# A five-layer graph GRU on one core: four batches in flight, and every state turned by block transpose and device memory instead of by TensorE

## The chip, the cores and the metric

The kernel runs on one core of a Trainium2 chip. The metric is device time in microseconds of one execution, as the median of several runs. Five engines work in parallel, each through its own queue in order, and wait for one another by semaphores: TensorE (PE, with its weight loads shown as PEld), VectorE (DVE), ScalarE (ACT), GpSimd (POOL), and SyncE (SP), which here only issues DMAs.

## The reference

For each of 16 batches with 512 nodes and 128 features: a normalized graph convolution, a residual and a layer norm; then five layers of message passing with a GRU, a residual and a layer norm.

```python
adj_norm = adj / (jnp.sum(adj, axis=-1, keepdims=True) + EPS)
h_neigh = jnp.einsum('bnm,bmf->bnf', adj_norm, x)
h = jnp.einsum('bnk,ko->bno', jnp.concatenate([x, h_neigh], axis=-1), weight) + bias
x1 = layernorm(x + relu(h))

A = (adj != 0)
h = x1
for l in range(5):
    m = jnp.einsum('bnd,de->bne', h, weight[l])
    agg = jnp.einsum('bij,bid->bjd', A, m)
    gi = agg @ w_ih.T + b_ih;  gh = h @ w_hh.T + b_hh
    r = sigmoid(i_r + h_r);  z = sigmoid(i_z + h_z);  n = tanh(i_n + r * h_n)
    h = (1 - z) * n + z * h
out = layernorm(x1 + h * mask)
```

## The kernel before

**Numbers in two parts.** Each float32 operand of a matmul is kept as a rounded part (`_hi`, made by a copy on ACT) and the rest (`_lo`, made by a subtraction on DVE or POOL). A product of two such numbers is three matmuls, one after the other into the same PSUM bank (`split_product`, L1157 to L1159). The edges are 0 or 1, so the sum over neighbours takes two groups of four matmuls: `tok_hi` (L1292), then `tok_lo` (L1299). The weight of a layer and `w_ih` are multiplied once ahead of everything into `wc`.

**Units.** One layer of one batch is a unit, 80 in all. A state `h` lies with features on partitions ([128, 512]); the sum over neighbours needs it with nodes on partitions. So each unit of layer 1 to 4 first turns its state: four 128x128 transposes on PE against `ident` (L1152) into `ps_tok`, from which ACT makes `tok_hi` and DVE `tok_lo`. A unit then is, on PE: the 8 matmuls of the sum, 9 of `state_products` (`ps_hn`, and the state's part of `ps_r` and `ps_z`), and 9 with `agg_hi`/`agg_lo` (the rest of `ps_r`, of `ps_z`, and `ps_in`). ACT makes `agg_hi`, `r_gate`, `z_gate` and the tanh in `ps_in`; DVE makes `agg_lo`, `r_hn`, two steps in `ps_in` and the new `h`; POOL makes `z_h` and the state's low part `h_lo`; ACT makes `h_hi`.

**Windows and slots.** The whole order is written out by hand, as one function `window(w)` per engine. A window has five slots, and each slot may hold a unit, `UNITS = ((0, 0), (1, 2), (2, 4), (0, 1), (1, 3))`: slot 0 takes layer 0 of the window's batch, slot 1 layer 2 of the batch before it, and so on, so that three batches are in flight. The last steps of a unit (tanh, new state, `h_hi`, `h_lo`) are done in the slot after it, and the state for the next slot's unit is turned between `state_products` and the nine `agg` matmuls of a slot (`next_turned`). The middle windows are one hardware loop; the first two (`FIRST_WINDOWS`) and the last (`LAST_WINDOWS`) hold fewer units.

**Work beside the units.** Window n also prepares batch n+1 (`prepares`): `adjt_hi` (ACT) and `adjt_lo` (POOL, L544) and the products `own_products` (PE, `ps_b[0]` and `ps_b[1]`) in slot 0; row sums of `adj` (ACT), neighbour sums (PE) and the edges (DVE, L948, four operations, two in slot 1 and two in slot 2) in slots 1 and 2; the residual `pre1` and its statistics (DVE) in slot 3; the norm to `x1` (DVE, L931, four operations), its parts, and its turn to the first state (`first_state`, PE into `ps_b[1]`, then `h[0]`, `h_hi[0]` by ACT and `h_lo[0]` by POOL) in slot 4. `own_products` of the next window writes over `ps_b[1]` and so waits for `s_h0`, which stands behind the copy of `ps_b[1]` to `h[0]`.

**The last state's way.** In the middle windows the state after layer 4 does not go through PE. DVE transposes its 32x32 blocks (L1131) to `last_blocks`; SP writes that to device memory (`passage`, L472), waits for the landing and reads it back by four DMAs (`last_rows`, L475), which puts the blocks in their places. DVE then multiplies by the mask and adds the residual (`pre2`, L976, four operations, in slot 1 of the next window), takes the statistics, and POOL writes `y_out`.

```python
sp.wait_ge(s_blocks, w.finished(1, 1))
sp.dma_start(passage[:], last_blocks[:]...).then_inc(s_passed, 16)
sp.wait_ge(s_passed, w.finished(16, 16))
for q in range(Q):
    sp.dma_start(last_rows[...], passage...[:, :, q, :]).then_inc(s_rows, 16)
```

SP's queue in a window: last state, `xt_in`, `adjt_in` (1 MB), output, `x_in`, `adj_in` (1 MB).

## Time and profile before

| | us |
|---|---|
| median of 3 runs | 625.32 (624.67 to 625.62) |
| the profiled execution | 624.76 |
| its span in the trace | 623.0 |
| one window of the loop | 37.0 |

The trace is of the profiled execution. Its span runs from the first to the last instruction; the 1.8 us around it belong to the time but not to the trace. Durations of PE's matmuls reach to a modelled end and overlap the next matmul, so the pace of PE is read from the starts. DVE and ACT overlap the ends of their operations a little too: two DVE operations of 0.69 us stand about 0.61 us apart.

### The profile page before, as it was taken

How to read it: one execution, taken by the hardware profiler on the slowest of the kernel's cores; microseconds unless marked ns; L12 is line 12 of the kernel's file. 1: busy time of each engine (PE TensorE's matmuls, PEld its weight loads, DVE VectorE, ACT ScalarE, POOL GpSimd, SP SyncE). 2: the span in 40 equal slices, each digit the busy share in tenths (PEclk: the TensorE clock that was granted, in tenths of full speed). 3: DMA queues.
4: the chain of work that ended last, by engine and by line, in shares of the span. 5: the costliest groups of instructions: out<-in, count | busy, mean ns of one | idle time of the engine just before them, and what ended most of it. 6: DMA issues, size and time to landing. Idle time of an engine off the chain costs nothing.

```text
span 623.0 us, 10141 instructions
## 1 busy us (share of the span) xinstructions
PE 604.4 (97%) x2877; PEld 492.6 (79%) x2877; DVE 515.1 (83%) x1177; ACT 411.3 (66%) x777; POOL 366.5 (59%) x299
## 2 busy tenths in 40 slices
PE   6999999999999999999999999999999999999993
PEld 5677888888888888888888888888888888887772
DVE  5987978897988879798897979889798887967677
ACT  4866776858667585766758576685866758564551
POOL 0644555757666575765658576576766657555343
PEclk9999999999999999999999999999999999999997
DMA  8531222231232323223231331333124131010101
GB/s 270 213 102 68 101 69 102 99 104 52 84 134 68 101 68 121 80 84 114 88 101 51 99 120 67 118 100 102 51 84 135 67 101 34 17 34 1 51 1 52
DMA packets 48080, 54.63 MB, mean 88 GB/s; under 512 B 2880, under 2 KB 27968, under 8 KB 48064
## 3 DMA queue, kind: packets, MB, share of 16 engines
q1 hardware_dynamic: 47792, 54.31, 26.3%
q8 instruction: 7, 0.11, 0.1%
q10 hardware_dynamic: 272, 0.13, 0.1%
q14 instruction: 9, 0.07, 0.0%
HBM read 46.57 MB, written 7.86 MB: 87 GB/s over the span
## 4 chain that ended last, share of the span: by engine, by line
PE 91%; DVE 4%; DMA 1%; ACT 1%; issue 1%; SPq 1%; POOL 0%; POOLq 0%; DVEq 0%
PE ps_tok L1292 12%; PE ps_tok L1299 12%; PE ps_r L1157 6%; PE ps_r L1158 6%; PE ps_r L1159 6%; PE ps_z L1159 6%; PE ps_z L1158 6%; PE ps_z L1157 6%; PE ps_tok L1152 5%; PE ps_b L1157 3%; PE ps_b L1158 3%; PE ps_b L1159 3%; PE ps_in L1157 3%; PE ps_hn L1159 3%; PE ps_in L1158 3%; PE ps_in L1159 3%
## 5 line engine op out<-in xcount | busy, mean ns | idle before, releaser
L594 POOL TENSOR_TENSOR h_lo<-h,h_hi 128x512 fp32r<-128x512 f32 x64 | 82.9, 1295 | 107.5 <-ACT h_hi L624 107.5
L604 POOL TENSOR_TENSOR z_h<-z_gate,h 128x512 f32<-128x512 f32 x80 | 110.0, 1374 | 43.1 <-ACT z_gate L801 43.1
L624 ACT ACTIVATE tok_hi<-ps_tok 128x512 fp32r<-128x512 f32 x63 | 37.7, 598 | 96.2 <-PE ps_tok L1152 96.2
L1292 PE MATMUL ps_tok<-edges,tok_hi 128*128 (+1 forms) x320 | 87.9, 397 | 0.7 <-ACT tok_hi L624 0.7
L1136 DVE SCALAR_TENSOR_TENSOR r_hn<-ps_hn,gru_bias,r_gate 128x512 f32<-128x512 f32 x80 | 59.9, 748 | 34.5 <-ACT r_gate L791 33.4
L1299 PE MATMUL ps_tok<-edges,tok_lo 128*128 (+1 forms) x320 | 87.7, 396 | 0.0
L724 ACT ACTIVATE ps_in<-ps_in,gru_bias 128x512 f32<-128x512 f32 x80 | 52.8, 660 | 52.8 <-DVE ps_in L1020 52.7
L544 POOL TENSOR_TENSOR adjt_lo<-adjt_in,adjt_hi 128x512 fp32r<-128x512 f32 x56 | 71.8, 1302 | 4.2 <-ACT adjt_hi L624 4.2
L1292 PEld LDWEIGHTS ps_tok<-edges,tok_hi 128*128 128x128 f32 x320 | 59.8, 188 | 15.4 <-ACT tok_hi L624 0.9
L1299 PEld LDWEIGHTS ps_tok<-edges,tok_lo 128*128 128x128 f32 x320 | 59.9, 188 | 14.8 <-DVE tok_lo L827 0.3
L827 DVE TENSOR_TENSOR tok_lo<-ps_tok,tok_hi 128x512 fp32r<-128x512 f32 x63 | 43.6, 692 | 27.9 <-ACT tok_hi L624 27.9
L1059 DVE SCALAR_TENSOR_TENSOR ps_in<-z_gate,ps_in 128x512 f32<-128x512 f32 x80 | 55.2, 690 | 11.9 <-ACT ps_in L724 10.6
L791 ACT ACTIVATE r_gate<-ps_r,rz_bias 128x512 f32<-128x512 f32 x80 | 54.9, 686 | 14.2 <-PE ps_r L1159 11.4
L1020 DVE TENSOR_TENSOR ps_in<-ps_in,r_hn 128x512 f32<-128x512 f32 x80 | 56.0, 700 | 8.0
L827 DVE TENSOR_TENSOR agg_lo<-ps_tok,agg_hi 128x512 fp32r<-128x512 f32 x80 | 55.0, 688 | 4.3 <-ACT agg_hi L624 4.3
L624 ACT ACTIVATE agg_hi<-ps_tok 128x512 fp32r<-128x512 f32 x80 | 47.9, 598 | 15.2 <-PE ps_tok L1299 14.1
L962 DVE TENSOR_TENSOR h<-z_h,ps_in 128x512 f32<-128x512 f32 x80 | 54.4, 680 | 1.2
L801 ACT ACTIVATE z_gate<-ps_z,rz_bias 128x512 f32<-128x512 f32 x80 | 55.0, 687 | 0.5
L624 ACT ACTIVATE h_hi<-h 128x512 fp32r<-128x512 f32 x77 | 48.1, 625 | 7.2 <-DVE h L962 7.1
L550 POOL TENSOR_TENSOR rstd<-var,minus_half 128x4 f32<-128x4 f32 x15 | 15.3, 1021 | 48.2 <-DVE var L925 48.2
L1152 PEld LDWEIGHTS ps_tok<-ident,h 128*128 128x128 f32 x252 | 30.7, 140 | 10.7 <-issue 2.3
L1152 PE MATMUL ps_tok<-ident,h 128*128 128x128 f32 x252 | 38.0, 273 | 0.7 <-DVE agg_lo L827 0.3
(146 smaller groups left out, 1574.2 us busy)
## 6 DMA issues: line engine op xcount, KB each, us to landing
adjt_in<-in_adj_t_dram SPq DMA_DIRECT2D x14, 1024.0 KB, 5.3
adj_in<-in_adj_dram SPq DMA_DIRECT2D x14, 1024.0 KB, 5.4
x_in<-in_x_dram SPq DMA_DIRECT2D x16, 256.0 KB, 2.8
xt_in<-in_x_t_dram SPq DMA_DIRECT2D x15, 256.0 KB, 2.6
out_dram<-y_out SPq DMA_DIRECT2D x15, 256.0 KB, 2.3
passage<-last_blocks SPq DMA_DIRECT2D x14, 256.0 KB, 2.0
last_rows<-passage SPq DMA_DIRECT2D x56, 64.0 KB, 2.0
adjt_in<-in_adj_t_dram SPq DMA_DIRECT2D x4, 256.0 KB, 4.6
```

The source lines that it names most:

```text
L544: nc.gpsimd.tensor_tensor(adjt_lo[:, j, :], adjt_in[:, j, :], raw(adjt_hi[:, j, :]), ALU.subtract).then_inc(s_adjt_lo, 1)
L594: nc.gpsimd.tensor_tensor(h_lo[new][:], h[new][:], raw(h_hi[new][:]), ALU.subtract).then_inc(s_h_lo, 1)
L604: nc.gpsimd.tensor_tensor(z_h[:], z_gate[:], h[own][:], ALU.mult).then_inc(s_zh, 1)
L624: return nc.scalar.activation(dst, src, ACT.Copy)
L827: return nc.vector.tensor_tensor(dst, src, raw(hi), ALU.subtract)
L1136: nc.vector.scalar_tensor_tensor(out=r_hn[:], in0=ps_hn[:], scalar=bhh_cols[:, 2:3], in1=r_gate[:], op0=ALU.add, op1=ALU.mult).then_inc(s_ ...
L1152: return nc.tensor.transpose(dst, src, ident[:])
L1157: nc.tensor.matmul(dst, lhs_hi, rhs_hi, start=start, stop=False)
L1158: nc.tensor.matmul(dst, lhs_hi, rhs_lo, start=False, stop=False)
L1159: return nc.tensor.matmul(dst, lhs_lo, rhs_hi, start=False, stop=stop)
L1292: nc.tensor.matmul(ps_tok[:], tok_hi[:, c * P:(c + 1) * P], edges_from(c, unit[0]), start=c == 0, stop=False)
L1299: last = nc.tensor.matmul(ps_tok[:], tok_lo[:, c * P:(c + 1) * P], edges_from(c, unit[0]), start=False, stop=c == C - 1)
```

## The change

What it does:

- Four batches are in flight: `UNITS = ((0, 0), (3, 4), (2, 3), (1, 2), (0, 1))`. A state is used four slots after its unit, in place of three.
- From window 3 to window 15 every unit in the slots 1 to 4 takes its state by the way that only the last state took: block transpose on DVE (`blocks`, one buffer), write to `passage{k}`, four reads into `rows{k}`. In the loop SP does this five times per window (`pass_on`), between its loads. PE turns no state there.
- `tok_hi` is then made by ACT from `rows{k}`, one slot ahead, right behind `agg_hi`; `tok_lo` by POOL, no longer by DVE.
- The mask is applied by ACT: four operations in slot 3, between `r_gate` and `z_gate`, into `ps_b[2]` (`masked_last_state`). DVE adds the residual in one operation (`pre2`), now in slot 0. The output comes one window later.
- The first residual is written back into PSUM (`ps_b[0]`) and not to `pre1`; its statistics all come after `agg_lo` of slot 3.
- The edges are made by two operations of 1024 elements in slot 1. The norm to `x1` is split: two operations before `agg_lo` of slot 4, two after.
- `first_state` on PE moves to between the `ps_r` and the `ps_z` matmuls of slot 4. The copy to `h[0]`, on which `s_h0` hangs, moves from slot 4 to slot 0 of the next window, behind `agg_hi` and `tok_hi`. `h_lo[0]` moves from POOL to DVE.
- The row sums write to one buffer of 512 and wait for one another.
- Windows 2 and 3 hold four units each, with slot 4 and slot 1 empty, and there is one window more at the end (20, not 19).

The core of the diff:

```diff
-UNITS = ((0, 0), (1, 2), (2, 4), (0, 1), (1, 3))
+UNITS = ((0, 0), (3, 4), (2, 3), (1, 2), (0, 1))
...
 FIRST_WINDOWS = (((0, 0), None, None, None, (0, 1)),
-                 ((0, 0), (1, 2), (0, 1), None, (1, 3)))
-LAST_WINDOWS = (((0, 0), (1, 2), (0, 1), (2, 4), (0, 2)),
-                ((2, 3), (1, 3), (2, 4), None, None),
-                (None, (2, 4), None, None, None))
+                 ((0, 0), (1, 2), (0, 1), None, (1, 3)),
+                 ((0, 0), (1, 2), (2, 4), (0, 1), None),
+                 ((0, 0), None, (2, 3), (1, 2), (0, 1)))
+LAST_WINDOWS = (((3, 4), (1, 2), None, None, None),
+                ((3, 3), (2, 3), (3, 4), None, None),
+                (None, (3, 4), None, None, None))
...
+def is_moved(batches, n, slot):
+    return 3 <= n < batches and slot > 0
...
# SP: one state's way
+            def pass_on(w, slot):
+                k = w.unit_before(slot)[1] + 1
+                sp.wait_ge(s_blocks, w.moved(slot))
+                sp.dma_start(passage[k][:], blocks[:].rearrange("p q c j -> p (q c j)")).then_inc(s_passed, 16)
+                sp.wait_ge(s_passed, w.value(lambda n: 16 * moved_states(B, n, slot)))
                 for q in range(Q):
+                    sp.dma_start(rows[k][q * SQ:(q + 1) * SQ, :, :, :].rearrange("i f c j -> i f (c j)"),
+                                 passage[k].rearrange("(f i) (q m) -> i f q m", f=Q, q=Q)[:, :, q, :]
+                                 ).then_inc(s_rows[k], 16)
...
# POOL
+                    if w.next_moved(slot):
+                        pool.wait_ge(s_tok_hi, w.turned(slot + 2))
+                        nc.gpsimd.tensor_tensor(tokens(tok_lo), rows_by_tokens(w.unit(slot + 1)[1]),
+                                                tokens(raw(tok_hi[:])), ALU.subtract).then_inc(s_tok_lo, 1)
...
-                    if slot == 4 and w.prepares() and not w.ramps():
-                        pool.wait_ge(s_h0_hi, w.prepared(1, 1))
-                        nc.gpsimd.tensor_tensor(h_lo[0][:], h[0][:], raw(h_hi[0][:]),
-                                                ALU.subtract).then_inc(s_h0_lo, 1)
...
# ACT
+                def masked_last_state():
+                    act.wait_ge(s_rows[LAYERS], w.rows(4 * 16, LAYERS))
+                    b = w.batch(3)
+                    for c in range(C):
+                        last = nc.scalar.activation(
+                            ps_b[2][:, c * P:(c + 1) * P].rearrange("p (f j) -> p f j", f=Q),
+                            rows[LAYERS][:, :, c, :], ACT.Copy, scale=mask_cols[:, bass.ds(b * C + c, 1)])
+                    last.then_inc(s_masked, 1)
...
+                    if w.next_moved(slot):
+                        k = w.unit(slot + 1)[1]
+                        act.wait_ge(s_rows[k], w.rows(4 * 16, k))
+                        evacuate(tokens(tok_hi), rows_by_tokens(k)).then_inc(s_tok_hi, 1)
+                    if slot == 0 and 3 <= w.first < B:
+                        h0_of_batch()
...
-                    if w.prepares() and slot == 4 and not w.ramps():
-                        h0_of_batch()
...
                     if w.prepares() and slot == 4 and not w.ramps():
-                        h0_hi_of_batch()
+                        h0_parts_of_batch()
+                    if slot == 3 and w.masks():
+                        masked_last_state()
...
# DVE
                         if slot == 4 and not w.ramps():
-                            norm1(w)
+                            norm1(w, (0, 1))
...
+                    if w.prepares() and slot == 4 and not w.ramps():
+                        norm1(w, (2, 3))
                     if w.prepares() and slot == 3 and not w.ramps():
-                        stats1_of((2, 3))
+                        stats1_of(w, range(C))
...
+                    if w.moves(slot):
+                        dve.wait_ge(s_h, w.units(slot))
+                        if w.first > 2 or slot > 0:
+                            dve.wait_ge(s_passed, w.value(lambda n: 16 * (moved_states(B, n, slot) - 1)))
+                        nc.vector.transpose(blocks[:].rearrange("p q c j -> p c q j"),
+                                            h[w.home_made(slot)][:].rearrange("p (c q j) -> p c q j", c=C, q=Q)
+                                            ).then_inc(s_blocks, 1)
...
# PE
+                            if w.finishes():
+                                pe.wait_ge(s_end_read, w.finished(1, 1))
                             neighbour_sums((0, 1), w.prepared(C, 0))
...
-                            pe.wait_ge(s_pre1, w.prepared(1, 0))
+                            if w.first > 2:
+                                pe.wait_ge(s_x1, w.prepared(C, 0))
                             pe.wait_ge(s_h0, w.prepared(1, 0))
                             own_products(0)
...
+                        pe.wait_ge(s_agg_lo, w.units(slot + 1))
                         gate(ps_r, 0, agg_hi, agg_lo, wi_hi, wi_lo, False, True).then_inc(s_r_sum, 1)
+                    if w.prepares() and slot == 4 and not w.ramps():
+                        first_state()
```

How the order changes at three places of the loop. PE in slot 2, from the last state products to the first `agg` matmuls, before (line numbers are those of each kernel; L1152 is the turn of a state):

```order
L1158 MATMUL ps_z<-h_lo,whh_hi 128x512
L1159 MATMUL ps_z<-h_hi,whh_lo 128x512
...
L1152 MATMUL ps_tok<-ident,h 128x128 [waits s_h,s_agg_lo]
L1152 MATMUL ps_tok<-ident,h 128x128 x3
L1157 MATMUL ps_r<-agg_hi,wc_hi 128x512
L1158 MATMUL ps_r<-agg_lo,wc_hi 128x512
```

The same place after:

```order
L1259 MATMUL ps_z<-h_lo,whh_hi 128x512
L1260 MATMUL ps_z<-h_hi,whh_lo 128x512
...
L1258 MATMUL ps_r<-agg_hi,wc_hi 128x512 [waits s_agg_lo]
L1259 MATMUL ps_r<-agg_lo,wc_hi 128x512
L1260 MATMUL ps_r<-agg_hi,wc_lo 128x512
```

The turn is gone, and the wait for `agg_lo` stands at the `ps_r` matmuls themselves.

ACT from slot 4 over the end of the loop into slot 0, before (`h<-ps_b` is the copy on which `s_h0` hangs; the loop's first rows stand behind its last ones):

```order
L624 ACTIVATE tok_hi<-x 128x512 [waits s_x1]
...
L624 ACTIVATE x_kept<-x 128x512
L624 ACTIVATE h_hi<-h 128x512 [waits s_h]
L624 ACTIVATE h<-ps_b 128x512 [waits s_x1t]
L791 ACTIVATE r_gate<-ps_r,rz_bias 128x512 [waits s_rhn,s_r_sum]
L624 ACTIVATE h_hi<-h 128x512 [waits s_h0]
L801 ACTIVATE z_gate<-ps_z,rz_bias 128x512 [waits s_h,s_z_sum]
```

After, the end of slot 4, and then the start of slot 0:

```order
L689 ACTIVATE h_hi<-h 128x512 [waits s_h]
L870 ACTIVATE r_gate<-ps_r,rz_bias 128x512 [waits s_rhn,s_r_sum]
L689 ACTIVATE h_hi<-ps_b 128x512 [waits s_x1t]
L882 ACTIVATE z_gate<-ps_z,rz_bias 128x512 [waits s_h,s_z_sum]
```

```order
L689 ACTIVATE xt_hi<-xt_in 128x512 [waits s_xt_in]
...
L800 ACTIVATE ps_in<-ps_in,gru_bias 128x512 [waits s_npre]
...
L689 ACTIVATE agg_hi<-ps_tok 128x512 [waits s_agg]
...
L689 ACTIVATE tok_hi<-rows 128x512 [waits s_rows4]
...
L689 ACTIVATE h<-ps_b 128x512 [waits s_h0_lo]
L689 ACTIVATE adjt_hi<-adjt_in 128x512 [waits s_adjt_in]
```

The copy to `h[0]` now stands behind the tanh, `agg_hi` and `tok_hi` of slot 0.

POOL in slots 0 and 1 of the loop, after (before, the two `tok_lo` rows are not there):

```order
L609 TENSOR_TENSOR adjt_lo<-adjt_in,adjt_hi 128x512 [waits s_adjt_hi]
...
L655 TENSOR_TENSOR tok_lo<-rows,tok_hi 128x512 [waits s_tok_hi]
...
L664 TENSOR_TENSOR h_lo<-h,h_hi 128x512 [waits s_h_hi]
...
L669 TENSOR_TENSOR z_h<-z_gate,h 128x512 [waits s_z]
...
L609 TENSOR_TENSOR adjt_lo<-adjt_in,adjt_hi 128x512 [waits s_adjt_hi]
```

The row of `adjt_lo` stands twice in a row at each of its two places. `tok_lo` of slot 1's unit now comes behind the first two of them, and the other two behind it.

## Rows read from the trace of the kernel before

**Rows 1.** The page's first part: busy us, share of the span and instructions per engine.
```profile
PE 604.4 (97%) x2877; PEld 492.6 (79%) x2877; DVE 515.1 (83%) x1177; ACT 411.3 (66%) x777; POOL 366.5 (59%) x299
```

**Rows 2.** Busy time by stretch: us, PE, PEld, DVE, ACT, POOL; later rows PE alone; PEclk.
```profile
293.60:330.60 37.00, 37.00 (x180) 30.47 (x179) 31.61 (x73) 25.59 (x49) 23.89 (x20) 1.00 0.29 92
...
615.00:616.00 1.00, 0.28 (x3) 1.00 0.00 0
616.00:617.00 1.00, 0.00 (x0) 0.56 0.00 0
```

**Rows 3.** PE in order of time: start, us, line, operation, names; slot 0, then 3.
```profile
297.29 0.36 PE L1157 MATMUL ps_b<-w_hi,xt_hi 128*128 128x256 f32 x1
...
298.80 0.40 PE L1157 MATMUL ps_r<-agg_hi,wc_hi 128*128 128x512 f32 x1
...
317.02 1.10 PE L1292 MATMUL ps_tok<-edges,tok_hi 128*128 x4
...
320.73 0.39 PE L1159 MATMUL ps_z<-h_hi,whh_lo 128*128 128x512 f32 x1
320.96 0.60 PE L1152 MATMUL ps_tok<-ident,h 128*128 128x128 f32 x4
321.31 0.48 PE L1157 MATMUL ps_r<-agg_hi,wc_hi 128*128 128x512 f32 x1
321.63 0.40 PE L1158 MATMUL ps_r<-agg_lo,wc_hi 128*128 128x512 f32 x1
321.87 0.40 PE L1159 MATMUL ps_r<-agg_hi,wc_lo 128*128 128x512 f32 x1
...
323.49 1.10 PE L1292 MATMUL ps_tok<-edges,tok_hi 128*128 x4
```

**Rows 4.** ACT in order of time, slots 3 and 4 (in brackets: idle time before).
```profile
319.09 0.60 ACT L624 ACTIVATE agg_hi<-ps_tok 128x512 fp32r<-128x512 f32 x1
...
326.05 0.62 ACT L624 ACTIVATE tok_hi<-x 128x512 fp32r<-128x512 f32 x1
326.57 0.62 ACT L624 ACTIVATE x_kept<-x 128x512 f32 x1
...
328.28 0.58 ACT L624 ACTIVATE h<-ps_b 128x512 f32<-128x512 f32 x1
328.76 0.68 ACT L791 ACTIVATE r_gate<-ps_r,rz_bias 128x512 f32<-128x512 f32 x1
```

**Rows 5.** DVE in order of time, slots 1, 3 and 4.
```profile
304.79 1.14 DVE L976 SCALAR_TENSOR_TENSOR pre<-last_rows,mask_cols,x_kept 128x128 f32<-128x128 f32 x4
...
308.25 1.67 DVE L948 TENSOR_SCALAR edges<-adj_in 128x512 f32 x2
...
320.63 0.48 DVE L918 BATCH_NORM_STATS2 stats<-pre 128x6 f32<-128x128 f32 x2
321.14 0.69 DVE L962 TENSOR_TENSOR h<-z_h,ps_in 128x512 f32<-128x512 f32 x1
...
324.48 1.43 DVE L931 TENSOR_SCALAR x<-pre,mv,rstd 128x128 f32<-128x128 f32 x4
...
326.43 0.69 DVE L827 TENSOR_TENSOR agg_lo<-ps_tok,agg_hi 128x512 fp32r<-128x512 f32 x1
```

**Rows 6.** POOL in order of time, slot 1.
```profile
302.43 2.56 POOL L544 TENSOR_TENSOR adjt_lo<-adjt_in,adjt_hi 128x512 fp32r<-128x512 f32 x2
308.02 1.29 POOL L594 TENSOR_TENSOR h_lo<-h,h_hi 128x512 fp32r<-128x512 f32 x1 [3.03 <-ACT h_hi L624]
```

**Rows 7.** SP in order of time: the last state's write and its four reads.
```profile
291.39 0.35 SPq L472 DMA_DIRECT2D passage<-last_blocks  x1
293.44 1.76 SPq L475 DMA_DIRECT2D last_rows<-passage  x4
```

**Rows 8.** One line each of the tiles' views: duration ns min/median/max, first and last start.
```profile
L1131 DVE STREAM_TRANSPOSE last_blocks<-h x14: 701/707/708, 105.8 to 583.9; 128x512 f32<-128x512 f32 x14
L948 DVE TENSOR_SCALAR edges<-adj_in x56: 412/421/1443, 55.0 to 536.8; 128x512 f32 x48, 128x512 fp32r<-128x512 f32 x8
L604 POOL TENSOR_TENSOR z_h<-z_gate,h x80: 1262/1302/1756, 27.8 to 611.5; 128x512 f32<-128x512 f32 x80
```

**Rows 9.** DMA issues by line: count, KB each, median us from issue to landing.
```profile
adj_in<-in_adj_dram SPq DMA_DIRECT2D x14, 1024.0 KB, 5.4
last_rows<-passage SPq DMA_DIRECT2D x56, 64.0 KB, 2.0
```

270 lines of the change are left out of this document (151 added, 119 removed).

## The prediction

> **What bounds the kernel now.** Read first the busy shares: PE is busy 97% of the span [rows 1]. Then one window of the loop: PE is busy in all of it at a granted clock of 1.00, DVE in 31.6 of 37 us, ACT in 25.6, POOL in 23.9 [rows 2]. So a window lasts as long as PE has instructions to issue, and the other engines matter only where one of them is late for PE. Last read the starts on PE: they tell what an instruction costs there [rows 3]. Starts below are given from the first sum matmul of their slot; for slot 3 that is 317.02.
>
> **What leaves PE.** The state's turn starts at 320.96 and the next matmul at 321.31: 0.35 us. That matmul also takes 0.32 us to its successor at 321.63, where the next takes 0.24 to 321.87. A turn thus costs PE 0.35 + 0.09 = 0.44 us, not the 0.60 of its row [rows 3]. Units that no longer turn: three in window 3 (its slot 1 is empty) and four in each of the windows 4 to 15, together 51; one more batch at the end has its last state turned on PE. So 50 x 0.44 = **-22.0 us**. A window would go from 37.0 to 35.2. Nothing else leaves PE: `first_state` only moves.
>
> **Cover.** Between the end of a sum and its `agg` matmuls PE has 9 state products and had the turn; it came to the `ps_r` matmuls 321.31 - 317.02 = 4.29 after the slot's start, and will at 4.29 - 0.35 = 3.94. `agg_hi` starts 2.07 after the start and takes 0.60 [rows 4], so `agg_lo` can end at 2.70 + 0.69 = 3.4 [rows 5]. That still fits by 0.5, if DVE and ACT are free.
>
> **DVE.** Block transposes: four more per window at 0.71 [rows 8], against four `tok_lo` of 0.69 that go to POOL: about nothing. `h_lo[0]` comes, +0.6. `pre2` shrinks from 1.14 to about 0.7, the edges lose two starts. Each transpose waits for its own engine's `h`, 0.1 each. DVE stays near 32 of 35.2 us: not the bound, but with little slack. I cost it at nothing, except where it holds up ACT:
>
> **The chain that I expect PE to wait for.** In slot 3 all statistics now stand between `agg_lo` and `h`: 3.3 + four times 0.2 (the pair takes 0.48, the step to `h` 0.51 [rows 5]) puts `h` at 4.2 to 4.9. The transpose ends at 5.7, the moments near 6.2. ACT now has an `h_hi` in this slot (0.6, before `r_gate`): `r_gate` ends near 6.15. `r_hn` ends at 7.0, which is 1.0 into slot 4 (the slot is 6.47 - 0.44 = 6.03 long [rows 3]); the trace of before has it there at 0.3. In slot 4: `ps_in` at 1.1 to 1.8, tanh to 2.5, `agg_hi` to 3.0, `agg_lo` 3.1 to 3.8 (PE comes at 3.94: it fits by 0.1). The second half of the norm is then done at 4.5, half of 1.43 later [rows 5], where all of it was done at 2.4. ACT's `tok_hi<-x` starts there and not at 326.05 - 323.49 = 2.56 [rows 3, 4]; behind it stand, one after the other, `x_kept`, `h_hi`, `r_gate`, `h_hi[0]`, 0.5 to 0.7 each: they end at 7.3 (before, `r_gate` started at 328.76 - 323.49 = 5.3). DVE's `r_hn` and `h_lo[0]` follow, and its first step in slot 0 ends 2.3 after that slot's start. Then ACT in series: tanh 3.0, `agg_hi` 3.5, `tok_hi` 4.1, `h<-ps_b` **4.6**. PE wants to write `ps_b` at 3.94 and waits for this copy: **0.65 us per window**. Before, that copy ran at 328.28, in slot 4 [rows 4], long done. The bounds: if the norm's second half runs as early as it can, the copy ends at 4.1 and PE waits 0.2; if each of six ACT steps is 0.1 later, 1.25. `own_products` run beside it in the windows 4 to 14, eleven: 11 x 0.65 = **+7.2 us**.
>
> **POOL.** It gains four `tok_lo` and loses one `h_lo`: 23.9 + 3 x 1.3 = 27.8 of 35 us [rows 2, 6]. In slot 0 it is tight: `adjt_hi` is made from 4.5 on, two `adjt_lo` (2.56 [rows 6]) and `tok_lo` 1.3 end near 9.0; PE wants it at 4.6 + 1.51 (`own_products`, 297.29 to 298.80 [rows 3]) + 2.1 (nine matmuls) + 0.94 = 9.15. After `h_lo`, `z_h` and two `adjt_lo`, 5.2 us, the last `adjt_lo` is there at 14.2, and PE's fourth neighbour sum wants it at 14.2. Two fits with no slack: I take 0.1 per window, 11 x 0.1 = **+1.1 us**, bounds 0 and the rival below.
>
> **SP and the rows.** One way costs 2.05 from the write's issue to the reads' issue, 1.76 for the reads, 2.0 to land [rows 7, 9]: 5.8 us from the block transpose, and SP is held 3.9 of them, five times in 35 us. States for a next layer have 9 us of room: transposed at 4.7 of one slot, used at 2.6 two slots on. The tight one is the last state: transposed at 4.8 of slot 2, landed at 10.6, which is 4.1 of slot 3; ACT wants it after `r_gate`, at 6.1. It fits by 2 us, even behind the end of the 1 MB load of 5.4 us [rows 9]. The four masking operations, about 1.1 us on ACT, push `z_gate` to 1.9 of slot 4, just ahead of the tanh: cover, nothing on PE.
>
> **Ramp.** Windows 2 and 3 have a slot without a unit, and the same 80 units. In window 2 nothing covers the norm in slot 4: `ps_in`, two norms, tanh, DVE's next step and two norms end about 3.4 after PE ran dry; the turn, `tok_hi<-x` and POOL's low part then cost PE another 0.6. **+4.0 us**. In window 3, slot 1, PE has only neighbour sums, and the last two `adjt_lo` follow `z_gate` and `z_h` of slot 0 (1.3 each): **+2.1 us**. Bounds for both together: 3 and 9; a clock that falls after such a gap is in the upper one. The trace shows it at 1.00 through a gap of 3.2 us near the end and at 0.56 a microsecond after PE's last matmul [rows 2], with no work there to price it. The tail runs the same last ten units in the same order.
>
> **The sum.** 624.8 (span 623.0 and 1.8 around it) - 22.0 + 7.2 + 1.1 + 6.1 = 617.2 for an execution like the profiled one; the median is 0.5 above that: **617.7 us**.
>
> **A rule of the skill.** Two of the edge operations took 1.67 us, while `h_lo` ran on POOL until 309.31, and one alone takes 0.42 at least and 1.44 at most [rows 5, 6, 8]: the first waited 1.25 for POOL's end and then ran. The Trainium skill (SBUF — State Buffer, "SBUF: two separate sides") has it that a two-port operation of VectorE and one of GpSimd hold their shared ports as a lock, for the whole instruction. The trace agrees. With more work on POOL, both edge operations of slot 1 may each meet one of its operations.
>
> **Rivals.**
> (B) *The copy is in time and nothing else waits.* The chain above is a sum of twenty steps, each good to 0.05. For it: PE waited nowhere in the loop before, with DVE as busy. 617.7 - 8.3 = **609.4**. Chance 0.22.
> (C) *POOL becomes the bound in the slots 0 and 1.* It has seven operations between the first `adjt_hi` and PE's fourth neighbour sum, five before, and no slack. `z_h` was up to 1.756 against 1.302 [rows 8]. If its seven take 0.15 to 0.4 more each, PE waits 1.0 to 2.8 per window more: 11 x 1.0 to 2.8 on 617.7 - 1.1 gives 628 to 647; middle **633**. It decides from 0.7 us per window more than my forecast, 0.1 per operation. This is the slower side. Against it: the median of its operations is 1.30, and the 1.75 came beside one DVE operation. Chance 0.13.
> (D) *The edges meet POOL twice.* Each then waits up to 1.3, `r_hn` of slot 1 comes 1 us later, and so `agg_lo` of slot 2, for which I have 3.9 against PE's 4.4: 0.5 per window, **623**. Chance 0.14, on both sides of no change.
> (E) *The rows come late*, the reads of 512 bytes being slowed by the loads in flight: from 2 us late on, masking holds `z_gate`, the tanh and `agg_hi`. 1 us per window, 12 windows: **629**. Chance 0.05.
> (A) *The forecast*, 613 to 622: chance 0.46.
>
> **How the numbers follow.** About 0.2% (1.25 us) is what a measurement can tell from no change. Faster: A, B, nearly two thirds of D: 0.78. Same: a third of D, edges of A and C: 0.07. Slower: most of C, E, a bit of D: 0.15. The range takes in B with a lighter ramp, D and the near part of C: 607 to 629; each side leaves out about 0.1.
>
> **What would show it.** In a window of the loop: PE's idle time of 0.2 to 1.2 us ahead of `own_products`, released by ACT's `h<-ps_b`, and a length near 35.9; no idle time in the other slots above 0.2. For B: length 35.2. For C: PE waiting for POOL's `adjt_lo` or `tok_lo`, POOL busy over 30 us. For D: the two edge operations over 3 us together. For E: ACT's masking released by a DMA. In window 2, slot 4: a gap on PE of about 3.4 us released by DVE's norm. The sum is wrong if a turn was worth less than 0.44 because the wait for `agg_lo` takes its place; then the `ps_r` matmuls show idle time before them in each slot.

## The result and the profile after

| | before | after |
|---|---|---|
| median of 13 runs each | 624.66 us | 622.03 us |
| lowest to highest | 623.97 to 625.62 | 621.25 to 624.83 |
| profiled execution, its span | 624.76, 623.0 | 621.57, 619.4 |
| one window of the loop | 36.97 | 36.19 |

The ratio is 0.9964, with a 95% interval of 0.9953 to 0.9974: faster, by 0.36%. The forecast was 617.7 us in a range of 607 to 629, so the sign and the range held and the size did not: of 7 us expected, 2.6 came. Five of the 13 executions took 622.8 or more.

Below, a window is counted from the first sum matmul of slot 0 to the next one, and a slot likewise. Slot lengths in us, read from the starts on PE, for a usual window:

| kernel, a window of the loop | slot 0 | 1 | 2 | 3 | 4 | sum |
|---|---|---|---|---|---|---|
| before | 7.91 | 9.21 | 6.92 | 6.47 | 6.46 | 36.97 |
| after | 8.19 | 8.74 | 6.49 | 6.09 | 6.68 | 36.19 |
| after, if PE waited nowhere (before, less 0.44 for each turn) | 7.47 | 8.77 | 6.48 | 6.03 | 6.46 | 35.21 |

Four turns left each window, one from each of the slots 0 to 3. The slots 1 to 3 became 0.4 to 0.5 shorter, the price of one. Slot 0 lost its turn and became longer, by a wait; slot 4 had no turn to lose, and became longer too.

Busy shares of after, to be set beside [rows 1]: PE has 200 instructions less, DVE is as busy as before, ACT has 12 us more and POOL 43 us.

```profile
PE 591.6 (96%) x2677; PEld 470.2 (76%) x2677; DVE 516.7 (83%) x1124; ACT 423.8 (68%) x829; POOL 409.5 (66%) x337
```

One window, to be set beside [rows 2] (length, then busy time of PE, PEld, DVE, ACT, POOL, then PE's clock). PE now has half a microsecond in which it does nothing; the POOL column went from 23.9 to 27.2, where the forecast had 27.8.

```profile
282.99:319.18 36.19, 35.68 (x164) 28.48 (x162) 31.72 (x68) 26.38 (x53) 27.18 (x23) 1.00 0.47 151
```

What PE waited for in all of the span (total, times, longest). The first line is the eleven windows in which the next batch's `own_products` run; the other two are the ramp:

```profile
PE ps_b L1258 <- ACT h L689: 5.5, 11, 0.5
PE ps_b L1253 <- DVE x L1016: 3.6, 1, 3.6
...
PE ps_b L1258 <- POOL adjt_lo L609: 1.6, 2, 1.4
```

**Slot 0: the copy.** PE has nothing to issue from the last `ps_z` matmul on until ACT has copied `h` out of `ps_b`. On ACT each operation follows the one before, from a tanh that waited for DVE (idle time and releaser in brackets):

```profile
286.67 0.39 PE L1260 MATMUL ps_z<-h_hi,whh_lo 128*128 128x512 f32 x1
287.57 0.36 PE L1258 MATMUL ps_b<-w_hi,xt_hi 128*128 128x256 f32 x1 [0.51 <-ACT h L689]
...
285.25 0.66 ACT L800 ACTIVATE ps_in<-ps_in,gru_bias 128x512 f32<-128x512 f32 x1 [0.44 <-DVE ps_in L1114]
285.83 0.59 ACT L689 ACTIVATE agg_hi<-ps_tok 128x512 fp32r<-128x512 f32 x1
286.31 0.63 ACT L689 ACTIVATE tok_hi<-rows 128x512 fp32r<-128x512 f32 x1
286.83 0.59 ACT L689 ACTIVATE h<-ps_b 128x512 f32<-128x512 f32 x1
```

From one PE start to the next there are 0.90 us, where two neighbours of that kind are 0.23 or 0.24 apart: 0.66 us per window. The copy ends 287.42 - 282.99 = 4.43 after the slot's start; the forecast had 4.6 and a wait of 0.65.

**Slot 4: `agg_lo`.** The forecast let it fit by 0.1. It comes 0.2 late. First DVE from the middle of slot 3 (which starts at 306.40), then ACT across the border (slot 4 starts at 312.48), then PE:

```profile
308.83 0.70 DVE L1152 SCALAR_TENSOR_TENSOR ps_in<-z_gate,ps_in 128x512 f32<-128x512 f32 x1 [0.21 <-ACT ps_in L800]
309.43 0.68 DVE L908 TENSOR_TENSOR agg_lo<-ps_tok,agg_hi 128x512 fp32r<-128x512 f32 x1
310.03 0.88 DVE L1003 BATCH_NORM_STATS2 stats<-ps_b 128x6 f32<-128x128 f32 x4
310.95 0.69 DVE L1053 TENSOR_TENSOR h<-z_h,ps_in 128x512 f32<-128x512 f32 x1
...
312.20 0.67 ACT L870 ACTIVATE r_gate<-ps_r,rz_bias 128x512 f32<-128x512 f32 x1
312.78 1.23 ACT L775 ACTIVATE ps_b<-rows,mask_cols 128x128 f32<-128x128 f32 x4
313.94 0.67 ACT L882 ACTIVATE z_gate<-ps_z,rz_bias 128x512 f32<-128x512 f32 x1
...
315.80 0.68 DVE L908 TENSOR_TENSOR agg_lo<-ps_tok,agg_hi 128x512 fp32r<-128x512 f32 x1
...
316.18 0.39 PE L1260 MATMUL ps_z<-h_hi,whh_lo 128*128 128x512 f32 x1
316.54 0.51 PE L1258 MATMUL ps_r<-agg_hi,wc_hi 128*128 128x512 f32 x1
316.88 0.39 PE L1259 MATMUL ps_r<-agg_lo,wc_hi 128*128 128x512 f32 x1
```

From 316.18 the next start is 0.36 away, and the one after that 0.34, instead of 0.23 twice. These two small gaps are what the slot lost, 0.22 by its length. No bracket stands before 316.54, as the wait is shorter than what the view lists: it is seen in the starts alone.

**The ramp.** After the gap of 3.57 us that the forecast had at 3.4, the granted clock falls, about two microseconds after work has set in again (stretch, PE busy, then the clock):

```profile
104.00:106.00 2.00, 1.60 (x8) 0.99 0.64 188
106.00:107.00 1.00, 1.00 (x3) 0.50 0.87 206
107.00:108.00 1.00, 1.00 (x4) 0.50 0.83 217
...
109.00:110.00 1.00, 1.00 (x5) 0.81 1.03 389
```

0.50 is the lower of the two levels, 1.2 GHz. From window 2's `own_products` to window 3's there are 36.1 us, where the forecast's steps give 34.5 (30.5 of work and 4.0 of gap): 1.6 us. It named this fall, in the bound and not in the sum.

**DVE and the last state's write.** There is a wait that the forecast did not look at: DVE's block transpose writes a buffer that the previous state's write to memory may not yet have left.

```profile
DVE blocks L1183 <- DMA passage<-blocks: 2.4, 4, 1.6
```

Four times in 64; one of them (1.6 us) makes the only loop window of 36.35 instead of 36.19: DVE is late from there on, and the 0.16 comes out in slot 2, which takes 6.63. The forecast had followed the rows to ACT, and not the write back to DVE.

### The profile page after: what moved, and what is told of

Its sections match the earlier page's. It is cut to its first block, busy times and chain, and to the rows that moved or that the text cites. A ratio compares the mean times of both kernels' runs of the same rounds, so it can differ in the third digit from the quotient of the medians.

```text
span 619.4 us, 10053 instructions
## 1 busy us (share of the span) xinstructions
PE 591.6 (96%) x2677; PEld 470.2 (76%) x2677; DVE 516.7 (83%) x1124; ACT 423.8 (68%) x829; POOL 409.5 (66%) x337
## 4 chain that ended last, share of the span: by engine, by line
PE 32%; DVE 28%; issue 18%; ACT 18%; DMA 2%; POOL 1%; ACTq 1%; DVEq 1%; POOLq 0%
PE ps_tok L1397 5%; PE ps_tok L1390 4%; DVE ps_in L1114 4%; ACT ps_in L800 4%; DVE r_hn L1237 4%; DVE h L1053 3%; ACT tok_hi L689 3%; DVE edges L1033 2%; ACT ps_b L775 2%; ACT sum_of L701 2%; DVE ps_b L983 2%; DVE stats L1003 2%; PE ps_b L1258 2%; PE ps_r L1258 2%; PE ps_r L1259 2%
## 5 line engine op out<-in xcount | busy, mean ns | idle before, releaser
L669 POOL TENSOR_TENSOR z_h<-z_gate,h 128x512 f32<-128x512 f32 x80 | 108.0, 1351 | 29.6 <-ACT z_gate L882 28.2
L655 POOL TENSOR_TENSOR tok_lo<-rows,tok_hi 128x512 fp32r<-128x512 f32 x51 | 66.2, 1298 | 33.4 <-ACT tok_hi L689 33.4
L1152 DVE SCALAR_TENSOR_TENSOR ps_in<-z_gate,ps_in 128x512 f32<-128x512 f32 x80 | 55.5, 694 | 22.5 <-ACT ps_in L800 20.1
L689 ACT ACTIVATE h_hi<-h 128x512 fp32r<-128x512 f32 x64 | 40.0, 625 | 26.4 <-DVE h L1053 26.3
L1183 DVE STREAM_TRANSPOSE blocks<-h 128x512 f32<-128x512 f32 x64 | 45.6, 712 | 9.1 <-DMA passage<-blocks 2.4
L701 ACT ACTIVATE sum_of<-adj_in 128x512 f32<-128x512 f32 x57 | 36.0, 632 | 1.9 <-DMA adj_in<-in_adj_dram 0.5
L689 ACT ACTIVATE adjt_hi<-adjt_in 128x512 fp32r<-128x512 f32 x60 | 34.6, 630 | 1.4 <-DMA adjt_in<-in_adj_t_dram 1.4
```

Of the source, the lines that this page charges most:

```text
L655: nc.gpsimd.tensor_tensor(tokens(tok_lo), rows_by_tokens(w.unit(slot + 1)[1]), tokens(raw(tok_hi[:])), ALU.subtract).then_inc(s_tok_lo, 1)
L669: nc.gpsimd.tensor_tensor(z_h[:], z_gate[:], h[own][:], ALU.mult).then_inc(s_zh, 1)
L689: return nc.scalar.activation(dst, src, ACT.Copy)
L1152: nc.vector.scalar_tensor_tensor(out=ps_in[:], in0=z_gate[:], scalar=1.0, in1=ps_in[:], op0=ALU.subtract, op1=ALU.mult).then_inc(s_zm1n, 1)
```

## The experiments

The first four runs priced terms of the sum and the late write, one edit each. The chip ran the kernel before at 624.84 for them, 624.39 for the next four, 624.75 for the three after these and 624.86 for the last two.

### The copy earlier

```
@@ ACT, a slot's head @@
+                    if slot == 0 and 3 <= w.first < B:
+                        h0_of_batch()
                     if w.unit_before(slot):
                         act.wait_ge(s_npre, w.units(slot))
...
-                    if slot == 0 and 3 <= w.first < B:
-                        h0_of_batch()
```

> The changed kernel, with one edit on ACT: from window 3 on, the copy of ps_b[1] to h[0] stands in slot 0 ahead of the tanh, and not behind tanh, agg_hi and tok_hi. In the changed kernel's trace PE stands still ahead of own_products in eleven windows: 0.89 us from start to start in place of 0.23, released by this copy, which ends at 287.42. ACT sits idle for 0.44 us just before that tanh, so the copy should fit there and end about 1.5 us after the slot's start. Theory 1 (each window loses 0.66 us to this wait alone): windows go from 36.19 to 35.5, the execution from 622.0 to 614.8, a ratio to the kernel before of 0.984. Theory 2 (the wait is only the first of several that are nearly due, and POOL's adjt_lo and tok_lo or DVE's agg_lo take its place): windows of 35.9 to 36.1, 618.5 to 621, ratio 0.990 to 0.994.

Measured: 619.95 us (617.33 to 624.04), ratio 0.9924 with an interval of 0.9896 to 0.9952. PE's wait for the copy is gone. Slot 0 went from 8.19 to 7.46, slot 1 gave back 0.1, and the usual window is 35.70. That is 0.49 less, eleven times: 5.4 us. But the median gained only 2.1. The profiled execution shows why: two windows have a slot 2 of 7.84 and 8.16 instead of 6.55, and a slot in window 3 is 7.62 instead of 6.47. In both long slots 2 DVE had first waited for a late write (1.10 and 1.57 us) and was behind when it came to the edges, which then took 2.39 and 3.44 us instead of 1.26. The longer of the two:

```profile
513.23 3.44 DVE L1033 TENSOR_SCALAR edges<-adj_in 128x1024 f32 x2
```

So the copy wait is real and priced; something else, which comes and goes, takes back more than half.

### Work into the gap

```
+                    if w.first == 2 and slot == 4:
+                        for _ in range(38):
+                            turn(ps_tok[:, 0:P], ident[:])
                     if w.prepares() and slot == 4 and not w.ramps():
                         first_state()
```

> [...]
```profile
106.00:108.00 2.00, 1.87 (x9) 1.00 0.87 186
108.00:110.00 2.00, 2.00 (x10) 1.00 0.95 338
```

and the stretch from one `own_products` to the next is 34.72 instead of 36.11. In this pair of traces the fall of the clock thus cost 1.4 us, and the gap alone is worth what the forecast had for it, within 0.2. The medians are 1.0 apart, and that alone would not be clear of the noise. The price is not the same each time: in the eight traces of this study that have the gap and no turns in it, that stretch takes 35.4 to 36.5 us, so 0.7 to 1.8 more than with them.

### The turns back

```
+                    if w.next_moved(slot):
+                        if unit:
+                            pe.wait_ge(s_agg_lo, w.units(slot + 1))
+                        for c in range(C):
+                            turn(ps_tok[:, c * P:(c + 1) * P], ident[:])
```

> The changed kernel, with four transposes of ident into ps_tok put back on PE at each of the 51 places where a state's turn stood before; nothing reads them. Theory 1 (a turn costs PE 0.44 us wherever PE is what the others wait for): the 12 in slot 0 hide in the wait of 0.66 us for the copy, except for what they leave over, the other 39 cost 0.44 each: 39 x 0.44 = 17.2 us, 639 us, ratio 1.023. Theory 2 (the turn had hidden in waits for agg_lo that are there anyway, so that taking it away gained less than its pace): 627 to 633, ratio 1.004 to 1.013.

Measured: 635.32 us (634.74 to 635.77), ratio 1.0170 (1.0155 to 1.0185), between what the two theories had. Slots 8.13, 9.21, 6.93, 6.47, 6.46: the last four are those of the kernel before. In its slot 3 a turn stands where it used to:

```profile
309.50 0.60 PE L1253 MATMUL ps_tok<-ident 128*128 128x128 f32 x4
309.85 0.48 PE L1258 MATMUL ps_r<-agg_hi,wc_hi 128*128 128x512 f32 x1
310.17 0.39 PE L1259 MATMUL ps_r<-agg_lo,wc_hi 128*128 128x512 f32 x1
```

0.35 to the next start and 0.09 on the one after: the 0.44 of the forecast. In the slots 1 to 3 it is the whole difference. In slot 0 it costs nothing, as it lies in the wait for the copy; and in slot 4, which has no turn, the 0.22 of waiting is gone; I put that down to the longer slot 3, in which DVE and ACT can get ready. So a window is 1.0 and not 4 x 0.44 = 1.76 longer than in the changed kernel: the rest of what the turns' removal was worth went into these two waits.

### The loads ahead of the last state's way

```
                 if w.loads():
                     sp.wait_ge(s_pre1, w.prepared(1, 1))
                     load_x(b)
...
                     load_adj(b)
+                if w.moves(3):
+                    pass_on(w, 3)
```

> The changed kernel, with one edit on SP: the loads of x_in and adj_in stand ahead of the fourth state's way and not behind it, so that the 1 MB load no longer runs just ahead of the fifth state's write. In the trace of the changed kernel DVE's block transpose in slot 0 waited for the landing of that write in four windows (0.39, 0.16, 1.62 and 0.21 us), and the window with 1.62 is 0.16 longer than the others. Theory 1 (these late landings make the executions of 624 us, five of thirteen being above 622.5): the spread shrinks to about that of the kernel before, 1.5 us, and the median falls by 0.5 us to 621.5. Theory 2 (the landings are covered, and the spread comes from elsewhere, for instance from how long the clock stays low after the gap in window 2): no change of the median beyond 0.3 us, and executions near 624 remain.

Measured: 629.24 us, ratio 1.0081 (1.0064 to 1.0098), the opposite of what the first theory said. DVE now waits in ten windows, and PE behind it:

```profile
DVE blocks L1183 <- DMA passage<-blocks: 15.2, 10, 2.6
...
PE ps_hn L1258 <- DVE h_lo L908: 3.2, 6, 1.2
```

So a write of 256 KB that is issued behind a load of 1 MB lands late enough to stop DVE. It is a way in which the changed kernel loses time; how often it does there was still to be seen.

### The loads behind it, and a second buffer

```
                 if w.moves(4):
                     pass_on(w, 4)
+                if w.loads():
...
+                    load_adj(b)
```

> The changed kernel, with one edit on SP: the loads of x_in and adj_in stand behind the fifth state's way, and not ahead of it. It is the counterpart of the run that put them ahead of the fourth way, which had ten late writes in its trace (5.4 us and more from the issue to the landing, against 2.0), DVE waiting up to 2.56 us for them, and 629.2 us. Theory 1 (a write that is issued while the 1 MB load is in flight lands late, and by chance late enough for DVE to wait): now no write meets that load in the first 3 us, the trace has no wait of DVE for a landing in slot 0, the spread shrinks to some 1.5 us, and the median is 621.4, ratio 0.9948. Theory 2 (the order matters little, because some write meets the load wherever it stands: now the one of slot 0): waits of DVE for a landing move to slot 1, median 622 to 625.

Measured: 623.54 us (622.24 to 626.35), ratio 0.9989 (0.9976 to 1.0001). DVE's wait for a landing is down to one of 0.2 us, and yet the median is 1.5 above the changed kernel's. Part of it can be seen: one window of the trace takes 37.62, with a slot 2 of 7.89. The load of `adj_in` now comes last, ACT waits 0.43 for it, the row sums are late, and the edges take 2.36:

```profile
480.69 2.36 DVE L1033 TENSOR_SCALAR edges<-adj_in 128x1024 f32 x2
```

```
-        blocks = sb("blocks", [P, Q, C, SQ])
+        blocks_of = [sb("blocks", [P, Q, C, SQ])[:],
+                     second_adj[:, 0, :].rearrange("p (q c j) -> p q c j", q=Q, c=C)]
...
-            dve.wait_ge(s_passed, w.value(lambda n: 16 * (moved_states(B, n, slot) - 1)))
+            dve.wait_ge(s_passed, w.value(lambda n: 16 * (moved_states(B, n, slot) - (2 if slot == 0 else 1))))
```

> The changed kernel, with one edit on DVE and SP: the block transpose of slot 4 goes to a buffer of its own, so that the one of slot 0 need not wait until slot 4's write has landed. The DMAs stand in the same order. Theory 1 (the late write costs time only through DVE's wait for the buffer): no DVE wait for a landing in the trace, windows all of 36.2, spread about 1.5 us, median 621.4, ratio 0.9948. Theory 2 (a late write costs through the rows that come late, or through SP, which is held up for the next state): DVE waits no more, but executions near 624 remain and the median does not move.

Measured: 622.21 us (621.55 to 623.75), ratio 0.9969 (0.9957 to 0.9981), with no wait for a landing in its trace and every window of the loop at 36.17 to 36.20. The changed kernel has 622.03. The late writes cost it nothing in the median through DVE's wait; the executions of 622.9 and 623.75 are still there without them. That theory falls as the cause of the spread, as far as six executions show. Under the early copy the late writes did cost: they stood ahead of both long slots 2.

### Three edits together

The early copy, the second buffer and the 38 turns of the identity, in one kernel.

> The changed kernel with three edits at once: the copy to h[0] ahead of the tanh, the second buffer for slot 4's blocks, and the 38 dummy transposes in the gap of window 2. If the three costs are separate they add up: windows of 35.7 in place of 36.2 (11 x 0.5 = 5.4 us, as the trace with the early copy alone shows outside its late writes), 1.6 for the clock, 0.6 to 2 for the late writes: 613.5 to 614.5, ratio 0.982 to 0.984. If they overlap, so that the late writes only showed because the windows had become short: 616 to 618.

Measured: 619.20 us (618.31 to 621.25), ratio 0.9913 (0.9900 to 0.9926). Windows of 35.70, but three of them 1.5 to 1.7 longer; and the slot in window 3 takes 7.70 instead of 6.47. No write is late for DVE any more, so the long windows need another cause. First DVE and POOL in the window that starts at 247.37 and has a slot 2 of 8.21:

```profile
261.05 2.23 DVE L926 TENSOR_SCALAR row_eps<-row_sum 128x4 f32<-128x4 f32 x1 [0.48 <-ACT sum_of L702]
...
263.59 0.17 DVE L1086 TENSOR_SCALAR var<-mv 128x4 f32<-128x4 f32 x1
...
263.78 2.40 DVE L1034 TENSOR_SCALAR edges<-adj_in 128x1024 f32 x2
266.11 0.74 DVE L1238 SCALAR_TENSOR_TENSOR r_hn<-ps_hn,gru_bias,r_gate 128x512 f32<-128x512 f32 x1
...
260.68 1.33 POOL L656 TENSOR_TENSOR tok_lo<-rows,tok_hi 128x512 fp32r<-128x512 f32 x1
261.93 1.33 POOL L665 TENSOR_TENSOR h_lo<-h,h_hi 128x512 fp32r<-128x512 f32 x1
263.98 1.65 POOL L670 TENSOR_TENSOR z_h<-z_gate,h 128x512 f32<-128x512 f32 x1 [0.72 <-ACT z_gate L883]
```

and the same four operations of DVE, with two of POOL, in the next window, 37.33 later:

```profile
298.38 1.00 DVE L926 TENSOR_SCALAR row_eps<-row_sum 128x4 f32<-128x4 f32 x1 [0.50 <-ACT sum_of L702]
...
299.69 0.93 DVE L1086 TENSOR_SCALAR var<-mv 128x4 f32<-128x4 f32 x1
...
300.63 1.26 DVE L1034 TENSOR_SCALAR edges<-adj_in 128x1024 f32 x2
301.81 0.74 DVE L1238 SCALAR_TENSOR_TENSOR r_hn<-ps_hn,gru_bias,r_gate 128x512 f32<-128x512 f32 x1
...
298.04 1.32 POOL L656 TENSOR_TENSOR tok_lo<-rows,tok_hi 128x512 fp32r<-128x512 f32 x1
299.28 1.32 POOL L665 TENSOR_TENSOR h_lo<-h,h_hi 128x512 fp32r<-128x512 f32 x1
```

`row_eps` adds a constant to 4 numbers per partition and takes 0.16 us where POOL rests. Here it starts in the middle of POOL's `tok_lo`. In the second window it ends with it, at 299.38. In the first it ends at 263.28, with POOL's next operation: POOL has taken its turn twice. DVE is then half a microsecond later at the edges, the second of them meets `z_h`, `r_hn` is 1.6 later in its slot, and PE waits 0.81 for it and 0.41 for `agg_lo` behind it. This is rival D's mechanism with another first link. The edges took 2.4 or more in the two long slots 2 of the early copy alone as well, with no such `row_eps`: there a late write had made DVE late. `row_eps` took over 2.2 us in two windows of this trace, and these are its two long slots 2. In the third long window ACT's masking waited 1.4 for the rows, and PE 1.0 for the `z_gate` behind it.

The Trainium skill (SBUF — State Buffer, "SBUF: two separate sides") has the pair of ports as an exclusive lock that is held for a whole instruction, and says that who starts first gets it. The trace agrees for one instruction. It shows besides that a waiting operation of DVE does not always come next: 1.00 us in one window, 2.23 in the other, with the same operations of POOL around it.

### More norm work behind `r_hn`

On top of the three edits: in slot 3 the moments behind `r_hn` and `h_hi` behind `r_gate`; in slot 4 the whole norm behind `agg_lo`.

```
-                        if slot == 4 and not w.ramps():
-                            norm1(w, (0, 1))
...
-                            norm1(w, (2, 3))
+                            norm1(w)
```

> The kernel with the three edits, and the order of slots 3 and 4 changed: in slot 3 DVE makes the moments behind r_hn, and ACT makes h_hi behind r_gate; in slot 4 all of the norm to x1 stands behind agg_lo. In the changed kernel slot 3 lasts 6.09 and slot 4 6.68 us, where PE's own work is 6.03 and 6.46: PE waits for agg_lo of slot 4, whose chain begins with r_gate and r_hn of slot 3, 0.8 to 1.2 us late. Theory 1 (that chain is what costs 0.2 to 0.3 per window): slot 4 falls to 6.46, windows to 35.4, 3 us less than the kernel with three edits. Theory 2 (x1 now comes late: POOL's rstd, then all of the norm, and first_state waits for it in slot 4): slot 4 lasts 6.7 to 7.2, no gain or up to 4 us more.

Measured: 625.19 us (623.20 to 627.28), ratio 1.0013 (0.9995 to 1.0030). `agg_lo` is no longer late, and PE waits for the norm in its place:

```profile
PE ps_b L1257 <- DVE x L1022: 3.2, 12, 0.3
```

Slot 4 is 6.95 instead of 6.68, and three windows have a slot 2 of 8.2. The split of the norm in the change is the better of the two. So the chain through slot 3 is what made `agg_lo` late; taken out of it, the norm is late instead, and by more.

### The small operations in another form

```
-    nc.vector.tensor_scalar(row_eps[:], row_sum[:], ROW_EPS, None, ALU.add)
+    nc.vector.scalar_tensor_tensor(out=row_eps[:], in0=row_sum[:], scalar=ROW_EPS, in1=minus_half[:],
+                                   op0=ALU.add, op1=ALU.max)
```

and `var` likewise; once on the three edits, once on the changed kernel alone.

> Built on e7_three_edits. In its trace three windows were 1.5 to 1.65 us longer than the rest. In the one that starts at 247.37 the 128x4 row_eps on DVE ran 2.23 us (1.00 in its neighbour), across two operations of POOL instead of one; from there the edges' two operations started 0.48 later in their slot and took 2.40 for 1.26, beside POOL's z_h, r_hn came 1.63 late and PE waited. Here row_eps and var of the last norm are formed by scalar_tensor_tensor (an addition and a maximum with a negative constant, which changes no value) instead of tensor_scalar; the 128x512 operations of that form run beside POOL at their usual 0.7 us. Theory 1 (the tensor_scalar form waits for POOL's whole operation, and the long windows come from such a wait that POOL wins twice): row_eps and var take 0.17 to 0.2 in every window, edges never over 1.9, slot 2 is 6.6 in every window, the span falls by 3 to 5 us from 619.1, median 616 to 617.5. Theory 2 (it is the size, not the form: any small operation of DVE is held up beside POOL): row_eps stays at 0.9 to 1.0, long windows stay, 618.5 to 619.5. Theory 3 (with the small ones out of the way the edges start 1 us earlier and now meet h_lo and z_h both): edges 2.4 in most windows, slot 2 longer in most, 625 or more.

> The changed kernel with the two small DVE operations in the scalar_tensor_tensor form alone. Theory 1 (waits that POOL wins twice are what makes 5 of its 13 executions 622.8 or more): row_eps and var at 0.2, no execution over 622.3, a median of 621.0 to 621.6, every window 36.2. Theory 2 (these executions come from late writes of the state alone): the spread stays at 3 us, median 621.8 to 622.2, DVE waits for the passage as before.

Measured: 620.62 us (618.13 to 623.79), ratio 0.9935 (0.9910 to 0.9960), and 623.41 us (621.19 to 626.10), ratio 0.9983 (0.9969 to 0.9996). Theory 1 is wrong: the operation waits as before. The tile's line has minimum, median and maximum in ns; beside it stands the reciprocal that follows:

```profile
L926 DVE SCALAR_TENSOR_TENSOR row_eps<-row_sum,minus_half x16: 155/968/2225, 12.9 to 511.3; 128x4 f32<-128x4 f32 x16
L1228 DVE RECIPROCAL row_inv<-row_eps x15: 164/167/179, 31.3 to 513.4; 128x4 f32<-128x4 f32 x15
```

(from the kernel of the next run, which has the same form). I had judged the form by operations that read PSUM. With both inputs in SBUF it waits. The same page and section of the Trainium skill says so: an operation of VectorE with two SBUF inputs takes the ports too. But "any small operation waits" is wrong as well: the reciprocal never does, nor do the statistics and the block transposes, beside POOL or not. In that kernel and in the first of these two, the two windows with a `row_eps` over 2.2 us are the two with a slot 2 of 8.25. The trace of the second has no such window, though its median is 1.4 above the changed kernel's.

### The second gap

```
                         if slot == 1:
                             pe.wait_ge(s_own, w.prepared(2, 2))
+                            if w.first == 3:
+                                for _ in range(15):
+                                    turn(ps_tok[:, 0:P], ident[:])
                             neighbour_sums((2, 3), w.prepared(C, 0)).then_inc(s_nsum, 1)
```

> e9_small_forms with 15 turns of the identity more on PE in window 3, slot 1, ahead of the products that wait for adjt_lo (their result is read by nobody). In e7_three_edits the granted clock was 0.50 from 118 to 120 and 0.68 from 120 to 122, after waits of 1.37 and 0.23 there, and the sums of that slot took 7.70 for 6.47. Theory 1 (the gap lets the clock fall in some executions): clock 1.00 in all of 114 to 124, that slot 6.5, up to 1.2 less than e9_small_forms where that one's clock fell, and equal where it did not. Theory 2 (the clock falls there anyway, or the 15 turns delay the sums): equal, or up to 0.5 more.

Measured: 620.36 us (618.64 to 623.71), ratio 0.9935 (0.9911 to 0.9959). The kernel that it stands on kept its clock there in its own trace, and so both have this slot at 6.47: no difference to be seen. Of eleven traces with that wait of 1.4 us two had the fall (they are the long slots of window 3 under the early copy and under the three edits). Inconclusive on its price, 1.2 us where it happens.

### `row_eps` on ACT

```
+                            act.wait_ge(s_row_sum, w.prepared(C, C))
+                            nc.scalar.activation(row_eps[:], row_sum[:], ACT.Copy, bias=ROW_EPS).then_inc(s_rinv, 1)
...
-                    if w.prepares() and slot == 1:
+                    if w.prepares() and slot == 1 and w.first == 0:
                         row_inverse(w.prepared(1, 1))
+                    if w.prepares() and slot == 1 and w.first > 0:
+                        dve.wait_ge(s_rinv, w.prepared(2, 1))
+                        nc.vector.reciprocal(row_inv[:], row_eps[:]).then_inc(s_rinv, 1)
```

Once on the three edits with the second group of turns, once on the changed kernel with the second buffer. The edit also moves the reciprocal ahead of the moments; the two were not tried apart.

> e7_three_edits with the second group of identity turns of e10_second_warm, and the 128x4 addition row_eps moved from DVE to ACT, behind the row sums; row_inv (a reciprocal, 0.17 in all rows, beside POOL or not) goes ahead of the moments on DVE. What e9_small_forms left: the small addition of DVE waited for POOL in either form, 0.95 to 1.0 in eight windows and 2.23 in two, and these two are its two windows of 8.25 in slot 2. Theory 1 (a window is long where POOL wins twice against row_eps, and DVE then brings var and edges 0.5 too late past z_h): without row_eps DVE has room for one lost turn more; no edges over 1.9 in windows 5 and up, unless they start late; slot 2 is 6.6 in every window, the median 616.5 to 617.5, executions within 1.5 of each other. Theory 2 (it is not row_eps: var or the edges then lose in its place): edges of 2.4 and slot 2 of 8.2 stay in one or more windows, 618.5 to 620.5. Theory 3 (the operation on ACT delays h_hi and the gates by 0.2): every window 0.1 to 0.2 longer.

> The changed kernel with the second buffer of e6_two_blocks and row_eps on ACT as in e12_eps_on_act (no early copy, no identity turns). e6_two_blocks ran 621.55 to 623.75 with no wait for a landing left. Theory 1 (the executions over 622.5 have a window in which POOL wins twice): all executions 621.2 to 622.3, median 621.6. Theory 2 (they come from somewhere else): the spread stays at 2 us or more, median 621.8 to 622.5.

Measured for the first: **613.61 us** (612.81 to 614.77), ratio 0.9820 (0.9807 to 0.9834), the fastest kernel of this study, 8.4 us below the changed one. Every window of the loop is 35.60 to 35.66, the slots 2 are 6.46 to 6.50, and the view has PE busy in all of it:

```profile
280.55:316.20 35.65, 35.65 (x164) 28.48 (x162) 31.33 (x67) 26.60 (x54) 27.19 (x23) 1.00 0.49 154
```

Its starts say a little less. Slot 4 is still 6.68, as `agg_lo` is late there by the same 0.2, and the window is 0.4 above the 35.21 of PE's own work. DVE in it, and POOL:

```profile
294.60 0.18 DVE L1208 RECIPROCAL row_inv<-row_eps 128x4 f32<-128x4 f32 x1 [0.71 <-ACT row_eps L834]
...
295.09 0.20 DVE L1088 TENSOR_SCALAR var<-mv 128x4 f32<-128x4 f32 x1
295.27 2.38 DVE L1036 TENSOR_SCALAR edges<-adj_in 128x1024 f32 x2
297.58 0.74 DVE L1244 SCALAR_TENSOR_TENSOR r_hn<-ps_hn,gru_bias,r_gate 128x512 f32<-128x512 f32 x1
...
293.92 1.33 POOL L656 TENSOR_TENSOR tok_lo<-rows,tok_hi 128x512 fp32r<-128x512 f32 x1
295.18 1.33 POOL L665 TENSOR_TENSOR h_lo<-h,h_hi 128x512 fp32r<-128x512 f32 x1
297.23 1.59 POOL L670 TENSOR_TENSOR z_h<-z_gate,h 128x512 f32<-128x512 f32 x1 [0.72 <-ACT z_gate L885]
```

The edges take 2.38 us here, as long as in the bad windows of before. But they start 1.7 ahead of the slot's border (296.96) and not behind it, wait for `h_lo` in time that nobody needs, and let `r_hn` start at 297.58, 0.62 into the slot as in a good window, while `z_h` on POOL waits a little in its turn (1.59 for 1.33). So it is not the length of the edges that costs, but how late they start. I expected 616.5 to 617.5: the run before had two such windows in its trace of 618.64, and without 2 x 1.65 of them it is at 615.3; the profiled execution here took 614.77. The rest is in the medians: the executions of that kernel reached 623.71, and here they lie within 2 us.

Measured for the second: 622.11 us (620.81 to 622.42), ratio 0.9954 (0.9940 to 0.9967). The median is that of the changed kernel. None of its 5 executions is over 622.5, where 5 of the changed kernel's 13 were. That fits, and is too few to show it.

## Why the prediction was right and wrong

In the order of its steps; the numbers are those of the profiled execution, forecast 617.2, measured 621.57.

- **What leaves PE, -22.0.** Right: 0.44 per turn where it comes back in the slots 1 to 3, and windows whose own work is 35.21 where the text said 35.2.
- **The copy, +7.2.** Right: eleven waits of 0.66 for a forecast of 0.65, and the copy ended at 4.43 for 4.6. Taken away, a window falls by 0.49 (slot 1 gives a little back).
- **Other small waits, +1.1, the term that was too small.** The windows are 36.19 and not 35.96: 0.23 more, eleven times, +2.5. Beyond PE's own work and the 0.66 of the copy a window has 0.32 where the forecast had 0.1: 0.22 in slot 4, 0.06 each in the slots 0 and 3, and 0.03 less in slot 1. The large one is slot 4's `agg_lo`, of which the text says "it fits by 0.1". The step that failed is the first of "Cover": "`agg_lo` can end at 2.70 + 0.69 = 3.4". In slot 3 it ended at 310.11 - 306.40 = 3.7, as DVE's `ps_in` step is ahead of it and itself waited 0.21 for ACT. All that the chain hangs on it came 0.2 to 0.35 late: `h` started at 4.55 for 4.2, `r_gate` ended at 6.5 for 6.15, `r_hn` at 7.25 for 7.0, the tanh at 2.7 of slot 4 for 2.5, and `agg_lo` at 4.0 for 3.8 where PE came at 3.94. Two runs bear on this: with `h_hi` and the moments of slot 3 moved back `agg_lo` was in time, and so it was with a slot 3 longer by a turn. A fit by 0.1 at the end of a chain of twenty steps was worth no more than a coin; I gave it 0.1 us and should have given it what its bounds gave, 0.05 to 0.3. The two fits of POOL, costed in the same term, held: no wait for `adjt_lo` or `tok_lo` in the loop.
- **The ramp, +6.1.** The two gaps were 3.57 and 1.37 + 0.23, near the 3.4 and 2.1 with what follows them. From window 3's `own_products` to window 4's there are 31.98 us, where the forecast's steps give 31.9. The clock that fell after the first gap is the miss, +1.6 by the stretch, 1.4 by the run that kept it. It stood in the bound; the row of before with 0.56 a microsecond after PE's last matmul [rows 2] had spoken for it, and the other with 1.00 through 3.2 us against. This is the second term that failed: the ramp was costed at a clock of 1.00 throughout.
- **The head, the tail and what lies around the span**: -0.8, +0.4 and +0.4, not forecast.
- **One late write**: +0.2. "It fits by 2 us" was said of the rows on their way to ACT, and held in the changed kernel; the write's other end, DVE's next transpose, was not followed.

Together +2.5, +1.6, +0.2 and 0.0 are 4.3 of the 4.4 us. The median lies 0.5 above the profiled execution, as forecast.

Of the rivals, B (no wait, 609.4) did not come about in the change, but all the edits of the fastest kernel together lead most of the way there: 613.6. C did not: POOL is busy 27.2 of 36.2 us in a window and PE does not wait for it in the loop. D was right in its mechanism, though not in the changed kernel's own trace, where the edges take 1.26 in all eleven windows. Twelve windows of six other traces have a slot 2 of 7.8 to 8.3, and in all twelve the edges take 2.36 to 3.44: nine stand behind a `row_eps` of over 2.2, two behind a late write, one behind a late load. With `row_eps` on DVE that is 11 of the 55 loop windows traced with the early copy, and 1 of the 66 traced with the copy wait and without the turns back: the wait makes the loss rarer and does not rule it out. In its reading of the rows of before the text had the first edge operation wait 1.25; the two took 1.67, of which 2 x 0.42 is their own work, so it waited about 0.9. E: the masking waited for rows once, in one of the experiments.

**What stays open.** Why one execution of the changed kernel takes 621.3 and another 624.8 is not settled. Each trace is of one execution, and that of the changed kernel is of a good one. Two things in the traces have the right size. One is a long slot 2, 1.4 us in the run with the loads behind the fifth way, whose executions went up to 626.4. The other is the clock's fall in window 2, 0.7 to 1.8 us. Neither can be the whole: with the clock kept two of eight executions were above 624; with DVE's wait for late writes taken away two of six were still above 622.5; with `row_eps` taken away as well none of five was. That the small forms alone have 623.4 in the median, with a trace in which every window is 36.2, is not explained; the interval of their ratio still overlaps that of the changed kernel.

## What to carry to other kernels

A wait on the bound engine hides what lies behind it: take one away and the next appears. Here 5.4 us were won in the windows and 3.3 of them were lost again elsewhere. Read the executions' spread as a symptom, look for single long windows, and compare one operation by operation with its neighbour. A tiny operation on an engine that shares ports with another costs the other's whole instruction, sometimes two; move it, or move it ahead to where its waiting costs nothing, before anything is made faster. And where a chain ends with "it fits by 0.1", charge its bounds and not zero.

## What the runs showed of the hardware

- Beside a POOL operation of 1.3 us, DVE's 128x4 `row_eps` and `var` took 0.85 to 1.0 us in most windows (0.17 alone), `row_eps` in nine windows of four traces 2.23 to 2.25. Of the operations of DVE that ran beside POOL, those that read PSUM, the statistics, the block transposes (711 to 715 ns in all 64) and the reciprocals (162 to 180 ns in all) took the same time as alone.
- 38 turns of the identity, whose result nobody reads, kept the clock at 1.00 where a gap of 3.57 us was followed by 0.50. The stretch around them took 1.4 us less than in the changed kernel's trace, and 0.7 to 1.8 less than in the eight traces with the gap.
- After the same pair of short waits in window 3 (1.37 and 0.23 us) the clock fell to 0.50 in two traces, and stayed at 1.00 in the nine others that have these waits.
- A write of 256 KB landed 2.0 us after its issue in the median. In the changed kernel's loop the one that is issued right behind the 1 MB load landed 4.5 to 7.2 us after it; with that load ahead of the fourth state's way DVE waited for a landing ten times, for up to 2.6 us.
